# Two transformer layers on one core: route weights broadcast by DMA instead of by matmul, routes turned after the attention stretch, in-place sums, and the wait for part of the weights moved

## The reference, cut to what matters

```python
xn = layernorm(x)                                   # x: 4 batches x 1024 tokens x 128
x  = x + attn0(xn, R) + moe0(xn)                    # causal attention, one head of 128; 16 experts of 64, top 2, + shared
xn = layernorm(x)
x  = x + attn1(xn) + block1(xn)                     # attn1: 16 heads of 8, no mask
# block1: 16 rotary heads of 4, causal; res = xn + o @ w_up; then 8 experts of 256, top 2, on rmsnorm(res)

# moe: each token has a route weight for each expert, zero for all but its two best
route = zeros(T, E).at[arange(T)[:, None], topk_idx].set(topk_w)
eo    = einsum('etm,emh->eth', silu(g) * u, w_down)
out   = einsum('te,eth->th', route, eo) + shared
```

## Time and profile before

| | |
|---|---|
| median of 3 runs | 2189.83 us (2189.42 to 2191.34) |
| the profiled execution | 2192.12 us |
| its span | 2190.3 us, 1.8 us less than its time |
| PE, DVE, ACT busy | 2070.0, 1559.5, 1218.0 us |
| mean granted TensorE clock | 0.968 of full |

### The profile page before, as it was taken

How to read it: one execution, slowest core, us unless ns; L and a number is a source line. 1 busy time by engine, 2 the same in 40 slices (tenths; PEclk the granted TensorE clock), 3 DMA queues, 4 the chain that set the end, 5 groups by cost and what they waited for, 6 DMA issues and landing times.

```text
span 2190.3 us, 33681 instructions
## 1 busy us (share of the span) xinstructions
PE 2070.0 (95%) x12072; PEld 962.2 (44%) x12072; DVE 1559.5 (71%) x2854; ACT 1218.0 (56%) x2329; POOL 130.8 (6%) x251
## 2 busy tenths in 40 slices
PE   5968999999999999998999999999999999999889
PEld 3622333435665233343666423343566533334355
DVE  5668887746779887673778888774677987867154
ACT  1323777774431677776342467777443166777621
POOL 2000011100000000110000000110000000111000
PEclk9956999999999999999999999999999998999989
DMA  4060100100042101000013210010004210000000
GB/s 156 1 173 1 30 16 26 31 2 1 1 116 64 35 5 36 16 17 1 1 58 82 44 30 16 26 31 2 1 1 116 61 25 14 21 26 17 1 0 10
DMA packets 46983, 71.75 MB, mean 33 GB/s; under 512 B 7968, under 2 KB 17120, under 8 KB 46432
## 3 DMA queue, kind: packets, MB, share of 16 engines
q1 hardware_dynamic: 46816, 69.61, 12.2%
HBM read 46.25 MB, written 22.54 MB: 31 GB/s over the span
## 4 chain that ended last, share of the span: by engine, by line
PE 87%; DVE 6%; ACT 3%; issue 2%; DMA 1%; SPq 0%; POOL 0%; DVEq 0%; ACTq 0%
PE ps L1550 18%; PE ps L1525 16%; PE ps L1494 16%; PE ps L1416 8%; PE ps L1393 8%; PE ps L1426 7%; DVE row_max L1045 3%; PE ps L1560 2%; PE ps L1345 2%; PE ps L1333 1%; ACT prob L1239 1%; PE ps L1314 1%; PE ps L1527 1%; PE ps L1339 1%; PE ps L1444 1%
## 5 line engine op out<-in xcount | busy, mean ns | idle before, releaser
L1239 ACT ACTIVATE prob<-ps 128x512 f32<-128x512 f32 (+3 forms) x1792 | 867.4, 555 | 350.5 <-PE ps L1525 261.1
L1045 DVE TENSOR_REDUCE row_max<-ps 128x1 f32<-128x1024 f32 x512 | 604.7, 1219 | 94.1 <-PE ps L1494 93.4
L1525 PE MATMUL ps<-q_stack,k_stack 96*128 96x512 bf16 (+4 forms) x1792 | 553.3, 363 | 22.8 <-ACT prob L1239 17.0
L1494 PE MATMUL ps<-k_stack,q_stack 96*128 96x512 bf16 (+4 forms) x1792 | 534.1, 373 | 17.9 <-DVE row_max L1045 8.9
L1042 DVE CUSTOM_DVE_ANT_0 tmp<-ps,const_b 128x128 f32<-128x128 f32 (+7 forms) x512 | 371.4, 756 | 131.6 <-PE ps L1494 118.2
L1550 PE MATMUL ps<-prob,v_ones 128*32 128x512 f32 (+3 forms) x3584 | 438.1, 561 | 2.5 <-ACT prob L1239 2.5
L1525 PEld LDWEIGHTS ps<-q_stack,k_stack 96*128 96x128 bf16 (+1 forms) x1792 | 172.3, 98 | 359.5 <-ACT prob L1239 230.5
L1494 PEld LDWEIGHTS ps<-k_stack,q_stack 96*128 96x128 bf16 (+1 forms) x1792 | 152.1, 99 | 362.3 <-DVE row_max L1042 94.0
L1182 ACT ACTIVATE prob<-ps 128x512 f32<-128x512 f32 x128 | 76.4, 597 | 295.6 <-PE ps L1416 295.5
L1393 PEld LDWEIGHTS ps<-wd,prob 128*128 128x128 f32 (+1 forms) x1600 | 207.1, 191 | 59.4 <-issue 39.1
L1393 PE MATMUL ps<-wd,prob 128*128 128x128 f32 (+1 forms) x1600 | 212.9, 276 | 4.1 <-DVE prob L950 4.1
(11 more groups left out here) (178 smaller groups left out, 1555.0 us busy)
## 6 DMA issues: line engine op xcount, KB each, us to landing
k_stack<-scratch_k SPq DMA_DIRECT2D x48, 256.0 KB, 6.5
q_stack<-scratch_q SPq DMA_DIRECT2D x48, 256.0 KB, 7.1
scratch_k<-tmp SPq DMA_DIRECT2D x36, 256.0 KB, 2.6
k_stack<-scratch_k SPq DMA_DIRECT2D x96, 64.0 KB, 2.2
q_stack<-scratch_q SPq DMA_DIRECT2D x96, 64.0 KB, 2.2
scratch_k<-tmp SPq DMA_DIRECT2D x36, 128.0 KB, 2.4
scratch_q<-tmp SPq DMA_DIRECT2D x12, 256.0 KB, 2.4
xx<-in_x SPq DMA_DIRECT2D x4, 512.0 KB, 4.1
```

What stands on the lines that cost most here:

```text
L1045: dve.tensor_reduce(nm[G % 2][:, t, j:j + 1], ring_pair(r)[:], AX_X, ALU.max).then_inc(s["ring_used"], 1)
L1239: act.activation(p_slot(v, j)[:, lo - at:hi - at], bank(UNIT_BANKS[u % 3])[:, 0:hi - lo], ACT.Exp, scale=SCALES[kind_of(G)]).then_inc(s["p ...
L1494: ins = pe.matmul(ring_pair(r)[:, lo:hi], queries(G, j)[:, t * P:(t + 1) * P], keys(G, j)[:, lo:hi], start=True, stop=True)
L1525: ins = pe.matmul(dst[:, 0:hi - lo], keys(G, j)[:, kc * P:(kc + 1) * P], queries(G, j)[:, lo:hi], start=True, stop=True)
```

## The change

1. `top2` writes the routes as one f32 tile (`routes`, no bf16 parts). The memsets of `routes` and the selection matrices `sel0`, `sel1` in `const_b` (1088 and 1024 of its 3264 columns) are gone.
2. The routes are turned by PE in f32 with 8 transposes (`turn_routes`): those of mixture 0 as an item of the ring, `front_routes`, copied by DVE into `routeT`. For batches 1 to 3 it stands behind the last item of the attention stretch; for batch 0 it is inside the first mixed stretch. Those of mixture 1 are turned as `turn_r` within `closing`, copied by ACT; in the last stretch before `turn_h`.
3. SP stores `routeT` to DRAM (`routes_out`) and reads each expert's row back on all its partitions (`spread_in`): 16 loads a mixture, two DMAs each for mixture 0 and one for mixture 1, into four slots `spread_w` of 128x512 f32. A load waits until the step that last read its slot is done. After an attention stretch `routes_out` and the first four loads stand in SP's order.
4. `spread` on DVE multiplies `gu` with `spread_w`, both in SBUF; the `spread` matmuls are gone. The shared expert's step writes `hid` directly and has no multiplication. The freed bank 3 is a second gate bank (`G_BANKS`).
5. Three token buffers `x_of` take the place of `xx` and two `x1`; both mixtures' sums are added in place, and the statistics of the second layernorm are an item of their own (`summed`).
6. At the start the wait for weights is split: PE waits for four loads (`experts`) before the first mixed stretch, for the other 14 after mixture 0; the first routes (`route0` on) go into the planner's stretch. GpSimd clears `k_stack` only when the first normalisation is done (`x_norm_ready`).
7. The planner's terms follow (gate may be two steps ahead), so the orders of all engines are made anew.

```diff
-    sel0 = np.zeros((P, (E0 + 1) * M0))
-    sel1 = np.zeros((P, E1 * P))
-    for a in range(PARTS):
-        for e in range(E0 + 1):
-            sel0[CW * a + e, e * M0:(e + 1) * M0] = 1.0
-        for e in range(E1):
-            sel1[CW * a + e, e * P:(e + 1) * P] = 1.0
-    cb = np.concatenate([np.eye(P), mask_wide, sel0, sel1], axis=1)
+    cb = np.concatenate([np.eye(P), mask_wide], axis=1)
...
-PAIRS = (3, 2)
+PAIRS = (2, 3)
...
+    def load_of(self, b, which, n):
+
+        half, c = divmod(n, CHUNKS[which])
+        if which == 1:
+            return LOADS_OF * self.mixtures.index((b, which)) + n // 2
+        return LOADS_OF * self.mixtures.index((b, which)) + half * (C0 - 1) + c if c < C0 - 1 else None
...
+    def first_routes(w):
+
+        at = chain(w, "front", 0, "DVE", (("route0", 1.6), ("route1", 1.0), ("route2", 0.9), ("route3", 1.2), ("route4", 0.4)))
+        at = w.op("DVE", ("front_routes", 0), 1.1, w.op("PE", ("front_routes", 0), 1.0, at))
+        return w.op("SP", ("routes_out", 0, 0), 0.5, at, lands=2.3)
...
-                at = do("PE", "gate", 0.88, last(taken), last(scaled), last(ups), xT if n == 0 else None, *(freed if n == 0 else ()))
+                at = do("PE", "gate", 0.88, last(taken, 2), last(taken) if n == 1 else None, last(scaled, 2), last(ups), xT if n == 0 else None, *(freed if n == 0 else ()))
...
-                hids.append(do("DVE", "spread", 0.7, scaled[-1], at, last(downs), last(hids)))
+                load = plan.load_of(b, which, n)
+                while load is not None and load > loads[-1][0]:
+                    loads.append(spread_in(w, loads[-1][0] + 1, loads, routed))
+                at = [at for k, at, _ in loads if k == load]
+                hids.append(do("DVE", "spread", 0.7 if at else 0.05, scaled[-1], last(downs), last(hids), *at))
+                for k, _, readers in loads:
+                    if k == load:
...
+    def spread_in(w, load, loads, routed):
+
+        which = plan.mixtures[load // LOADS_OF][1]
+        freed = [at for k, _, readers in loads if k == load - SPREADS for at in readers]
+        at = w.op("SP", ("spread_in", load), (0.9, 0.45)[which], routed, loads[-1][1] if loads else None, *freed, lands=3.0)
+        return load, at, []
...
-        turned = do("ACT", "turn_h", 1.1, do("PE", "turn_h", 1.0, shift))
-        routed = chain(w, "after", b, "DVE", (("weights", 0.8), ("top0", 0.9), ("top1", 1.0), ("top2", 0.9), ("top3", 1.2), ("top4", 1.6)), e)
+        routed = chain(w, "after", b, "DVE", (("weights", 0.8), ("top0", 0.9), ("top1", 1.0), ("top2", 0.9), ("top3", 1.2), ("top4", 0.4)), e)
+        if b == B - 1:
+            turned_r = do("ACT", "turn_r", 1.1, do("PE", "turn_r", 1.0, routed))
+        turned = do("ACT", "turn_h", 1.1, do("PE", "turn_h", 1.0, shift, turned_r if b == B - 1 else None))
         project = do("DVE", "project", 1.3, do("PE", "project", 2.0, turned))
...
+        if b < B - 1:
+            turned_r = do("ACT", "turn_r", 1.1, do("PE", "turn_r", 1.0, routed, project))
+        routed = w.op("SP", ("routes_out", b, 1), 0.5, turned_r, lands=2.3)
+        return xT, routed, turned_r, joined
...
+        if b == 0:
+            mixed = w.op("DVE", ("weights",), 0.1, mixed)
+            w.op("PE", ("weights",), 0.0, mixed)
+        first_sum = w.op("DVE", ("summed", b, 0), 0.9, half_mixed, tiled[T // 2 - 1])
+        mixed = w.op("DVE", ("summed", b, 1), 0.9, mixed, tiled[-1], first_sum)
...
-    for item in front(0):
+    for item in front(0)[:FRONT_FIRST.index("route0")]:
         plan.put(*item)
-    plan.add("weights")
...
+        if b + 1 < B:
+            plan.put(*turned)
+            plan.put("routes_out", b + 1, 0)
+            for n in range(SPREADS):
+                plan.put("spread_in", at + n)
...
-        xx = sb("xx", S)
+        x_of = [sb(f"x{n}", S) for n in range(3)]
...
-        routeT = sb("routeT", S, BF16)
-        routes = [sb(f"routes{n}", T * PARTS * CW, BF16) for n in range(2)]
-        rt = [r[:].rearrange("p (t a e) -> p t a e", a=PARTS, e=CW) for r in routes]
+        routeT = sb("routeT", S)
+        routes = [sb(f"routes{n}", T * EXPERTS[n]) for n in range(2)]
+        spread_w = [sb(f"spread_w{n}", HALF) for n in range(SPREADS)]
...
-        G_BANK, U_BANK, Y_BANK, SPREAD_BANK = 0, 1, 2, 3
+        G_BANKS, U_BANK, Y_BANK = (0, 3), 1, 2
...
+            def routes_out(b, which):
+                if which == 0:
+                    sp.wait_ge(s["ring_used"], ROUTES_RING[b] + 1)
+                else:
+                    sp.wait_ge(s["rt_ready"], b + 1)
+                if b:
+                    sp.wait_ge(s["hid_ready"], plan.step0[b - 1, which] + 2 * CHUNKS[which])
+                sp.dma_start(scratch_r[which], routeT[0:EXPERTS[which], :]).then_inc(s["routes_stored"], 16)
+
+            def spread_in(load):
+                (b, which), i = plan.mixtures[load // LOADS_OF], load % LOADS_OF
+                half, c = divmod(i, LOADS_OF // 2)
+                dst, tok = spread_w[load % SPREADS], slice(half * HALF, (half + 1) * HALF)
+                sp.wait_ge(s["routes_stored"], 16 * (routed_before(b, which) + 1))
+                if load >= SPREADS:
+                    sp.wait_ge(s["hid_ready"], LAST_STEP[load - SPREADS] + 1)
+                if which == 1:
+                    sp.dma_start(dst[:], scratch_r[1][c, tok].partition_broadcast(P)).then_inc(spread_loaded[load % SPREADS], 16)
+                else:
+                    for n in range(2):
+                        sp.dma_start(dst[M0 * n:M0 * (n + 1), :], scratch_r[0][2 * c + n, tok].partition_broadcast(M0)).then_inc(spread_loaded[load % SPREADS], 16)
+
...
+            pool.wait_ge(s["x_norm_ready"], 2)
...
-                        st.done(dve.scalar_tensor_tensor(left, key, scale, wide(col(6)), ALU.mult, ALU.mult))
-                        st.wait()
-                        for part in range(PARTS):
-                            dst = rt[which][:, :, part, 0:experts]
-                            ins = dve.tensor_copy(dst, left)
-                            if part == PARTS - 1:
-                                ins.then_inc(s[("route_ready0", "route_ready1")[which]], 1)
-                                break
-                            st.done(ins)
-                            st.wait()
-                            st.done(dve.tensor_tensor(left, left, dst, ALU.subtract))
-                            st.wait()
+                        dst = routes[which][:].rearrange("p (t e) -> p t e", e=experts)
+                        dve.scalar_tensor_tensor(dst, key, scale, wide(col(6)), ALU.mult, ALU.mult).then_inc(s[("route_ready0", "route_ready1")[which]], 1)
...
+            def front_routes(r, b):
+                dve.wait_ge(s["ring_psum"], r + 1)
+                if routed_before(b, 0):
+                    dve.wait_ge(s["routes_stored"], 16 * routed_before(b, 0))
+                dve.tensor_copy(routeT[0:E0, :], ring_pair(r)[0:E0, :]).then_inc(s["ring_used"], 1)
...
+                    dst = gu
+                    if n % C0 == C0 - 1:
+                        dst = hid
+                        dve.wait_ge(s["down_done"], k - 1)
...
-                dve.wait_ge(s["spread_psum"], spread_count(b, which, n))
+                if load is None:
+                    dve.wait_ge(s["hid_ready"], k)
+                    dve.sem_inc(s["hid_ready"], 1)
+                    return
+                dve.wait_ge(spread_loaded[load % SPREADS], spread_count(load))
                 if k >= 2:
                     dve.wait_ge(s["down_done"], k - 1)
-                dve.tensor_tensor(hid[k % 2][0:m, :], gu[k % 2][0:m, :], bank(SPREAD_BANK)[0:m, :], ALU.mult).then_inc(s["hid_ready"], 1)
+                dve.tensor_tensor(hid[k % 2][:], gu[k % 2][:], spread_w[load % SPREADS][:], ALU.mult).then_inc(s["hid_ready"], 1)
...
-                    dve.wait_ge(s["y_used"], plan.half0[b, 0] + half + 1)
-                    half_statistics(norms[1], x1[b % 2], half)
+                    dve.wait_ge(x_loaded, 16 * b + 16)
+                    if attended[b]:
+                        dve.wait_ge(s["o0_used"], b * T + attended[b])
+                    added[b] += 1
+                    dve.tensor_tensor(x[:, tok], x[:, tok], bank(Y_BANK), ALU.add).then_inc(s["y_used"], 1)
                 else:
-                    dve.tensor_tensor(res[:, tok], x1[b % 2][:, tok], bank(Y_BANK), ALU.add).then_inc(s["y_used"], 1)
+                    dve.tensor_tensor(res[:, tok], x[:, tok], bank(Y_BANK), ALU.add).then_inc(s["y_used"], 1)
                     dve.wait_ge(s["y_used"], plan.half0[b, 1] + half + 1)
                     dve.sem_inc(s["out_ready"], 1)
+
+            def summed(b, half):
+
+                dve.wait_ge(s["o0_used"], b * T + (half + 1) * T // 2)
+                dve.wait_ge(s["y_used"], plan.half0[b, 0] + half + 1)
...
+            def turn_routes(dst, which):
                 for t in range(T):
```

(38 more changed lines are left out.)

196 lines of the change are left out of this document (103 added, 93 removed).

## The result

| | before | after |
|---|---|---|
| median | 2189.83 us (5 runs, 2189.42 to 2191.53) | 2177.56 us (5 runs, 2176.65 to 2180.89) |
| ratio | | 0.9945 [0.9932, 0.9957] |
| span of the profiled execution | 2190.3 | 2175.7 |

The change makes the kernel 12.3 us faster. The forecast was 2165. The direction and the range held, the size did not: half of the gain is missing.

The account below looks back on a forecast made before the run. PE was taken to bound the kernel, busy 95% of the span, with DVE full in the third part. From 2192.1, -12.9 (middle), -10.7 (start) and -1.3 (last) gave 2167.2, a median of 2165 us; range 2150 to 2184.

Parts of the forecast that it names:

- The start: Start to the last down of the first mixed stretch: ends at 97.5 against 108.2 us, -10.7, between -14 and -5.
- The last stretch: Last mixed stretch: -3.3 us for spreads, +2.0 for later routes, so -1.3, between -3.5 and +1.
- The middle stretches: Three mixed stretches between attention stretches: -4.3 us each, -12.9 in all, between -25 and 0.
- second mixture's start: Middle stretch: mixture 1's routes come some 3 us later through DRAM, mostly covered; 1.0 us lost, between 0 and 3.
- PE's balance of -6.3: PE's work in a middle stretch: -7.2 us spreads, -0.9 bf16 turning, +1.8 f32 turning.
- The second gate bank: Middle stretch: a second gate bank takes 0.75 us off PE's 3.9 us of idle time.
- Steady loads: Spread loads within the mixtures: four slots give 16 to 24 us of lead, so cost 0.
- The border: From attention to a mixed stretch: turning and copying routes adds 0.85 us of PE idle time, between 0 and 2.2.
- DVE's third part: Third part of a middle stretch, where DVE is full: half of 1.7 us of removed spreads is lost, +0.9.
- The one whose number came closest, 2176: Rival: DVE and DRAM latency leave -1.5 us a middle stretch, start -9, last 0; 2176 us, chance 0.19.
- Late loads: Rival: spread loads queued behind twelve stack loads stop DVE in middle stretches; slower, 2204 us, chance 0.07.
- All PE work counts: Rival: gaps close too, middle stretches -7.5 us each, start -13, last -3; 2151 us, chance 0.15.

Follow-up runs that it names:

- e5_memset: The changed kernel with GpSimd's three memsets of k_stack back at the start; 2184.05 us, ratio 0.9966 to the kernel before.
- e9_two: The changed kernel; mixture 1's second gate no longer waits for DVE's first product, and the planner takes first stack loads to land after 9 us; 2162.08 us.
- e10_onebank: e6_all with one gate bank, gate and planner waiting as in the kernel before; 2156.27 us, ratio 0.9836.
- e7_nospread: The kernel before, orders unchanged, issuing only the first spread matmul of each mixture (7 of 136), later route weights left out; 2174.52 us.
- e1_gate: The changed kernel, but PE's second gate of mixture 1 no longer waits for DVE's product of step 0; 2166.46 us.
- e6_all: The changed kernel with the edits of e1_gate and e2_near, and next-batch routes turned ahead of the attention stretch's last item; 2155.57 us.
- e2_near: The changed kernel with the planner taking the first stack loads to land after 9 us instead of 4; 2168.77 us, ratio 0.9906.

## Why the prediction was right or wrong

**The start: right**, -10.7 forecast for the end of the last `down`, -11.7 measured (96.47 for 108.14). Its terms: the memsets 3.0, measured 3.2 (DVE's `var` ends 3.6 sooner, 0.45 of it from the next term). `const_b` 1.6 was too much: DVE starts at 7.04 instead of 7.49, 0.45. The first multiplication at "about 35" comes at 35.98. The first gate at 23.78 misses the 19: the logits are through at 19.81 and not at 18.8, `encode` goes first, and it takes 3.67 us instead of the 1.98 us of later batches. The profile gives the clock as 1.00 there, so the rows don't show why it is slow. The sum held all the same, for it had PE idle for 5.5 us ahead of the first `down` anyway.

**The last stretch**: -1.3 forecast, -1.3 measured, but this agreement shows little: the changed kernel and e5_memset have the same order there and differ by 3.8 us.

**The middle stretches: wrong.** The step that failed is the sum of -4.3 for a middle stretch, in two terms for waits: the 1.0 us for the second mixture's start, and the old stack loads, which had no term at all. Measured is -0.35 by the mean. With both waits mended (e9_two) it is -8.1, so the work that was taken off PE was there to be gained, and more of it than I had put.
- *PE's balance of -6.3* had the right sign and was too small. In e10_onebank the stretches are 9.8 us shorter; there mixture 0's f32 turning (0.9) has left for the attention stretch, and 1.4 us of idle time went too (4.73 to 3.36). That leaves some 7.5. In the first middle stretch of e9_two, where the turning is still inside and the clock is 1.00, PE's busy time is 9.3 us less (193.97 for 203.27). Not each part of it is borne out: e7_nospread measured half of my price for a spread matmul in an unchanged order. Where the rest comes from, the new order or shorter overlaps, the runs don't tell. That the two waits hid a balance larger than mine was luck for my total.
- *"The second mixture's start ... two gates ahead cover most; I take 1.0"*: this place costs 4.4 us of idle time and the low clock behind it; e1_gate gives back 3.9 us of the stretch even though 1.8 us of wait remain. The cause of the 4.4 us is not the latency of the routes, as I had put it. The second bank did not let the second gate run ahead: for step 1 of mixture 1 the wait for ACT was replaced by one for DVE, and DVE's order had its product 4 us late. I had the diff's line for `last(taken) if n == 1` and costed the bank as a gain.
- *"The second gate bank takes away idle time, 0.75"*: on the whole run nothing is seen of it (e10_onebank against e6_all, 2156.3 and 2155.6), but the clock may hide a gain, as said there.
- *"Steady loads ... I take 0"* was right for the loads of the spreads: of 52.2 us that DVE stood idle ahead of these multiplications PE caused 50.5 and no DMA any. But it asked only after the new loads. The old ones, the stack loads, were not in the sum: the order wants them 13 us sooner, they are issued only 6.5 us sooner, and the planner's 4.0 us for their landing was now what decided. e2_near gives back 5.2 us a stretch, some 1 us of which the attention stretch takes again.
- *The border, 0.85*: 1.3 us of idle time beyond the turning. Right in size.
- *Two sums* were added up wrong, to no effect on the forecast. The terms for the routes' way through DRAM (0.3 + 2.3 + 0.9 + 2.3) make 5.8 us, not 6.3. And the lower end of a middle stretch, "no border cost, no late start, all idle gone", is at least -6.3 + 0.9 - 3.9 = -9.3 by its own terms, not -8.5; e10_onebank reached -9.8.
- *DVE's third part, +0.9*: not seen. From the first piece on PE is full, 80.28 of 80.49 us (620.10 to 700.59), and e10_onebank shortens the stretch with DVE's 159.9 us unchanged. The 2.2 us less of DVE was itself off: 160.3 to 159.8, because DVE's new copy of `routeT` (1.21 us) and the 9 ns more of each of 48 multiplications (0.4) were not counted against it.

**The rivals.** The one whose number came closest, 2176, named the full third part and four DMAs in sequence as the cause; neither shows, so it was near for a wrong reason. *Late loads* falls as put. *All PE work counts* (2151) describes the kernel once the gate's wait and the term for the stack loads are mended and the routes are turned ahead of the border: 2155.6 and 2156.3.

The Trainium skill (SBUF — State Buffer, "Who interferes with whom") has the running instruction hold the shared ports to its end. The trace agrees in e5_memset (9.87 and 13.34 against memset ends at 9.85 and 13.32), and the delay that I had thought possible among the routes happened in small: after the change, a `TENSOR_SCALAR` at 20.51 takes 0.38 us instead of 0.23 and ends at 20.89, where the second memset (from 13.85, 3.5 each) ends at 20.82. The 62 cycles that the Trainium skill (VectorE: DVE Perf Modes, "The TRN2 errata") would have taken off the multiplication from SBUF do not appear: 688 ns now (x192), 679 with PSUM.

## What to carry to other kernels

When a change takes work off the bounding engine, list every wait that its orders rest on and ask which now comes due sooner: here the old stack loads, with a landing time in the planner that had never mattered. When a buffer is doubled, read the condition of the first steps by hand: the branch for step 1 turned the gain into a wait for a busier engine. And keep the planner's terms the same as the semaphores: both gaps, of 4.4 and 3.0 us, were waits of which it knew nothing or too little, and mending these two took two lines and gave more than the change itself.

## What the runs showed of the hardware

The granted clock makes short gaps dear: after a PE gap of 4.4 us it was 0.51 in the next 4 us and 0.63 in the 4 us after them, and after one of 3.0 us it was 0.63 for 4 us. In e1_gate, where the order is unchanged, 2.5 us less of idle time made a middle stretch 3.9 us shorter.

Whether a gap costs the clock is not told by its length alone. At the same place, ahead of `turn_r` in the first middle stretch, PE waits for 1.83 us in e1_gate and 1.84 us in e6_all, and soon after 0.59 us in both. Behind that, the pair of `up` matmuls takes 1.12 us in e1_gate and the clock in 581 to 585 us is 1.00; in e6_all the pair takes 2.08 us, and the clock there is 0.68.

The same order of instructions can run at either level of the clock (1.2 and 2.4 GHz). In the last stretch of the changed kernel the pair of `gate` matmuls of the second step takes 1.10 us:

```profile
2079.60 1.10 PE L1515 MATMUL ps<-tT,wg 128*128 128x512 f32 x2 [0.93 <-DVE prob L1029]
```

and in e5_memset, after the same wait of 0.93 us, 2.04:

```profile
2085.86 2.04 PE L1514 MATMUL ps<-tT,wg 128*128 128x512 f32 x2 [0.93 <-DVE prob L1028]
```

Its last stretch is 3.8 us longer for it (123.16 for 119.35). One profile can't tell a difference of 4 us there from none.
